# The first routing's operations two at a time in the second step beside attention A, its scatters one step earlier, and the second routing between the first expert tiles

## The reference

```
x = x + attn_a(layernorm(x))    # one head, rotary q and k, softmax, width 128
x = x + ffn(layernorm(x))       # 8 experts, each token goes to one of them
x = x + attn_b(layernorm(x))    # 16 heads of 64, causal
x = x + ffn(layernorm(x))       # the same experts again

def ffn(x):
    logits = x @ Wr + br
    idx = argmax(logits);  gates = softmax(logits)[idx]
    for ei in range(8):
        h = gelu(x @ W1[ei] + b1[ei]);  y = h @ W2[ei] + b2[ei]
        out += y * (gates where idx == ei)
```

## Time and profile before

| | |
|---|---|
| median of 3 runs | 865.49 us (863.0 to 867.37) |
| the profiled execution | 865.85 us, span from first to last instruction 863.5 us |
| busy: PE, DVE | 789.8 us (91%), 622.7 us (72%) |
| busy: ACT, POOL | 566.7 us (66%), 440.4 us (51%) |
| attention A with its loads | 0 to 122 us of the span |
| first experts | 123 to 226 us |
| attention B | 226 to 748 us |
| second experts | 748 us to the end |

### The profile page before, as it was taken

The page is one execution under the profiler, slowest core; times in us unless marked ns, Lnnn a source line. Parts: engine busy times, 40 slices in busy tenths (PEclk is TensorE's granted clock), DMA queues, the critical chain, the costliest instruction groups (busy, mean ns, idle before and its releaser), DMA issues.

```text
span 863.5 us, 24042 instructions
## 1 busy us (share of the span) xinstructions
PE 789.8 (91%) x6756; PEld 693.7 (80%) x6756; DVE 622.7 (72%) x2697; ACT 566.7 (66%) x2041; POOL 440.4 (51%) x771
## 2 busy tenths in 40 slices
PE   4999938999899999989999999999999999499992
PEld 3888827999778888878888888888778888399992
DVE  3889855666577777767777777887767776566664
ACT  1677645666577777767777777777767777266661
POOL 3334553677444454444544444544874544237772
PEclk9999957999999999999999999999999999889996
DMA  9920012313200000000000000000020000003135
GB/s 322 335 104 0 15 42 94 112 52 98 71 2 2 1 2 3 2 1 0 0 1 0 0 0 2 2 2 2 26 96 1 0 2 2 1 26 119 50 102 161
DMA packets 25928, 40.02 MB, mean 46 GB/s; under 512 B 4656, under 2 KB 17584, under 8 KB 24816
## 3 DMA queue, kind: packets, MB, share of 16 engines
q1 hardware_dynamic: 20848, 28.76, 10.4%
q0 software_dynamic: 4992, 10.27, 3.6%
HBM read 20.58 MB, written 18.43 MB: 45 GB/s over the span
## 4 chain that ended last, share of the span: by engine, by line
PE 75%; DVE 7%; POOL 7%; issue 6%; DMA 2%; ACT 1%; DVEq 0%; SPq 0%; POOLq 0%; ACTq 0%
PE PS L1151 11%; PE PS L1111 10%; PE PS L1163 10%; PE PS L1142 10%; PE PS L1120 9%; PE PS L1194 6%; PE PS L998 5%; PE PS L1000 5%; PE PS L999 5%; POOL xs_dram L323 2%; POOL w1b L356 1%; PE PS L1103 1%; PE PS L1048 1%; POOL pb L383 1%; POOL rstdA L318 1%
## 5 line engine op out<-in xcount | busy, mean ns | idle before, releaser
L381 POOL TENSOR_SCALAR pb<-pb,rib 128x128 f32<-128x128 f32 x256 | 96.1, 375 | 251.9 <-DVE rib L871 251.3
L862 DVE CUSTOM_DVE_ANT_0 PS<-PS,CST 128x128 f32<-128x128 f32 (+1 forms) x512 | 169.0, 381 | 65.3 <-PE PS L1163 62.0
L876 DVE COPY pT<-PS 128x384 f32<-128x384 f32 x256 | 139.7, 554 | 33.2 <-PE PS L1142 33.0
L522 ACT ACTIVATE pb<-PS,nbb 128x128 f32<-128x128 f32 x256 | 95.1, 371 | 102.4 <-DVE nbb L862 95.2
L496 ACT ACTIVATE yT<-PS,w1b 128x128 f32<-128x128 f32 x368 | 105.3, 369 | 64.8 <-PE PS L1111 64.8
L383 POOL TENSOR_SCALAR pb<-pb,rib 128x256 f32<-128x256 f32 x256 | 123.3, 482 | 0.0
L1142 PE MATMUL PS<-CST,pb 128*128 128x128 f32 x768 | 117.5, 279 | 4.4 <-POOL pb L383 3.6
L524 ACT ACTIVATE pb<-PS,nbb 128x256 f32<-128x256 f32 x256 | 121.4, 474 | 0.0
L339 POOL DMA_INDIRECT yt_dram<-XY x92 | 93.4, 1015 | 32.5 <-issue 19.7
L1142 PEld LDWEIGHTS PS<-CST,pb 128*128 128x128 f32 x768 | 85.8, 142 | 28.0 <-issue 15.3
L1151 PE MATMUL PS<-pT,vb 128*64 128x256 f32 (+1 forms) x1024 | 103.4, 339 | 1.9 <-DVE pT L876 1.6
(11 more groups left out here) (132 smaller groups left out, 1667.5 us busy)
## 6 DMA issues: line engine op xcount, KB each, us to landing
xs_dram<-XY SPq DMA_DIRECT2D x4, 1483.5 KB, 13.2
XY<-xs_dram SPq DMA_DIRECT2D x4, 1225.5 KB, 5.8
W1S<-in_W SPq DMA_DIRECT2D x1, 2048.0 KB, 21.3
W2S<-in_W SPq DMA_DIRECT2D x4, 512.0 KB, 8.3
out_dram<-X SPq DMA_DIRECT2D x8, 256.0 KB, 4.1
yt_dram<-XY POOLq DMA_INDIRECT x92, 2.4
XY<-xs_dram SPq DMA_DIRECT2D x4, 258.0 KB, 2.6
xs_dram<-TOK,POS POOLq DMA_INDIRECT x64, 2.4
```

The lines of the kernel that those rows point to most:

```text
L862: last = nc.vector.tensor_tensor_reduce(ps, ps, CST[:, m:m + c1 - c0], -SCALE_B, HIGHEST, ALU.add, ALU.min, nbb[:, hh % 4, c0 // P:c0 // P ...
L876: nc.vector.tensor_copy(pT[:, hh % 4, :], PS[:, bank, 0:3 * P]).then_inc(b_pT, 1)
```

## The change

The first routing's 28 operations are placed in two steps instead of three: 13 in step 13 (one at each of the first seven hooks, none at the eighth, two at each of the last three) and the other 15 in step 14, two at a time. POOL's wait for the routing moves from step 15 to step 14, and the scatters of group 0 are 2, 2, 3, 3, 3 and 3 in steps 14 to 19, with none in step 20. In the first expert layer the second routing gets the order that the second layer has: expert steps 0 to 6 behind every fourth operation; and the scatters of group 1 get the second layer's pace. The work itself is the same.

```diff
@@ gpsimd
             attn_a(ROUTE0_AT - 1, 0)
             for s in range(ROUTE0_AT, NB + 5):
                 attn_a(s, s % 2)
-                if s == ROUTE0_AT + 2:
+                if s == ROUTE0_AT + 1:
                     before_scatters(0)
@@ vector
-            def attn_a(s, u, parts=()):
+            def attn_a(s, u, parts=(), so_many=(0,) * HOOKS):
                 v = (u + 1) % 2
+                hook = iter(so_many)
 
                 def part():
-                    for _ in parts:
-                        return
+
+                    for _ in range(next(hook)):
+                        next(parts, None)
...
             parts = route(0)
-            for s in range(ROUTE0_AT - 1, NB + 5):
-                attn_a(s, s % 2, parts if s >= ROUTE0_AT else ())
-                if s == ROUTE0_AT + 2:
-                    for _ in parts:
-                        pass
+            attn_a(ROUTE0_AT - 1, 0)
+            attn_a(ROUTE0_AT, 1, parts, (1, 1, 1, 1, 1, 1, 1, 0, 2, 2, 2))
+            attn_a(ROUTE0_AT + 1, 0, parts, (2,) * HOOKS)
+            for _ in parts:
+                pass
+            for s in range(ROUTE0_AT + 2, NB + 5):
+                attn_a(s, s % 2)
                 if s >= NB + 1:
                     weight_parts(s - (NB + 1))
...
-SCATTERS_A = (0, 0, 2, 2, 3, 3, 3, 3)
+SCATTERS_A = (0, 2, 2, 3, 3, 3, 3, 0)
+
+HOOKS = 11
...
-STEP_BEHIND = ((22, 26, 28), (4, 8, 12, 16, 20, 24, 28))
-
-SCATTER_PACE = (tuple(2 + t for t in range(GT)), tuple(7 + 3 * t // 4 for t in range(GT)))
+STEP_BEHIND = ((4, 8, 12, 16, 20, 24, 28),) * 2
+
+SCATTER_PACE = (tuple(7 + 3 * t // 4 for t in range(GT)),) * 2
```

## The result

The changed kernel takes 868.19 us (866.06 to 871.03, 17 runs) and the kernel before 865.46 us (863.0 to 869.31, 17 runs, measured together): ratio 1.0034, 95% interval 1.0021 to 1.0047. By the ratio it is slower by 2.9 us (2.7 by the medians). The interval lies clear of no change, but the difference is smaller than the 0.5% that the prediction set as its border, so it counts as the same. The forecast was 869.7. The profiled execution has a span of 866.2 us for 863.5.

What follows compares the result with a forecast made beforehand. PE bounds the kernel nearly everywhere, DVE the routing steps of attention A; +5.4 to the second routing, -2.6 at the experts' start and +1.4 in the tiles make +4.2 us, 869.7 us on the median of 865.49, range 865.4 to 872.0.

Steps and rivals of the forecast that it cites:

- Step 13: Attention A's step 13 issues 13 routing operations for 11: +0.5 us (0.2 to 0.7).
- Step 14: Attention A's step 14 issues 15 routing operations for 11, ten ahead of the rotation: +2.2 us.
- The clock: PE's longer idle time in step 14 drops its clock to half, slowing step 15: +1.6 us.
- step 15's emptier hooks: Attention A's step 15 has six routing operations fewer, going from 5.8 to about 5.7 us: -0.1.
- the upper end: Clock stays low for the 5.2 us that the first experts need, costing 2.6 us instead of 1.6.
- The scatters: Step 16's third scatter delays POOL's power in step 17: +1.2 us (0.9 to 1.3).
- T: Start of the second routing, 123.04 us before the change, forecast to come 5.4 us later.
- The start of the experts: DVE waits 2.4 us for data; first expert matmul at T + 9.0 instead of T + 11.6: 2.6 us gained.
- The tiles: First expert tiles give back 1.1 us to routing operations between them and 0.3 us to close scatters.
- Sum: Whole kernel: +5.4 - 2.6 + 1.4 = +4.2 us.
- The two rivals that would have given less: Clock stays up in step 14: 868.1 us, chance 0.2; not slower, variance within 0.3 us: 865.5 us, chance 0.2.
- the first of them: Clock stays up in step 14 because PE's idle time stays short: +2.6, 868.1 us, chance 0.2.

Runs made afterwards that it cites:

- kernel with the pairs later: Changed kernel with step 14's last five routing operations moved from ahead of the row maximum to the hooks behind it; ratio 1.0030 to the kernel before.
- the filler: Changed kernel with 28 throwaway identity transposes on PE in its idle time between its work of steps 14 and 15; ratio 1.0046 to the kernel before.
- the routing part alone: Changed kernel with only attention A's routing and scatter change, the experts' order and pace as in the kernel before; ratio 1.0052 to the kernel before.

## Why the prediction was right

- **Step 13** (+0.5): 8.60 for 7.97, +0.6. Counted from X, the layer norm comes 0.2 us later, behind the operation that moved behind `nba`; the rotation's sum 0.5 later, behind the next hook's pair; the last hook's pair adds 0.1.
- **Step 14** (+2.2): +2.1. The variance came 0.9 us later for 1.1, and so did POOL's multiply counted from X (4.43 us for 3.57), and the small operation behind the rotation was held to its end. The kernel with the pairs later shows that the total is right and one reason in it is not: I put 0.7 us on the row maximum's lost cover and took the operations between the rotation and the row maximum as its cause. With these moved away the cover is lost all the same and the step is as long. That the ten ahead of the rotation are the cause is my reading of the rows. The Trainium skill, SBUF — State Buffer, section Who interferes with whom, has the rule for the hold (one of the two fully blocks, whichever comes second). The 1.03 us of L781 for its 0.17, and the 1.02 and 1.05 of `nbF` for 0.15, agree with it.
- **The clock** (+1.6, and -0.1 for step 15's emptier hooks): +0.8 together. It fell as forecast; the term was mis-sized. I took half of 3.2 us as lost in full; PE still idled in the first 0.5 of it, and against the filler step 15 lost 0.9. The other 2.9 us at half speed are 1.45 us of work by the same estimate; why only 0.9 of it shows, no run says. The execution of the routing part alone comes near the size that I had as the upper end (2.6): 8.0 us, +2.3 against the filler's 5.7.
- **The scatters** (+1.2): +1.24, step 17 from 6.52 to 7.76. Step 18 kept its length, 5.27 for 5.28, and so did the stretch from step 19's X to T, 6.84 for 6.83.
- **T** (+5.4): +4.9.
- **The start of the experts**: data 3.57 us behind T for 3.67, wait 2.32 for 2.4, first matmul T + 9.01 for T + 9.0. Gain 2.6, as said. Here the second layer was a faithful model of the first.
- **The tiles** (-1.1 and -0.3): four tiles on 9.88 us for 10.05, so -0.9; at attention B's first power -0.9 in all. The close scatters cost nothing more, and POOL caught up ahead of attention B (0.74 us idle at 224.73). The 0.5 that I had too much stands there.
- **Sum**: 4.9 - 2.6 + 0.9 = 3.2 us at attention B, for a forecast of 4.2 and a measured 2.9 over 17 runs. The two terms that were too large are the clock (0.7) and the tiles (0.5); the misses of steps 13 and 14 cancel.

The two rivals that would have given less fell at their own marks: the clock did fall, and the variance of step 14 came 0.9 us later, not within 0.3. The time alone couldn't have decided it: 868.19 us is what the first of them forecast (868.1), and only the clock rows and the filler's trace rule it out.

## What to carry to other kernels

Gaps of another stage take only so much work. Spread over three steps the 28 operations cost DVE's steps 20.2 us in all; in two steps and one without, the same three steps took 22.9 even with the clock kept up by the filler. Moving five of them to other gaps of step 14 changed its length by 0.05 us: how many there are decided, not where they stood. Before an indirect DMA is issued earlier, look at the issuing engine's idle time in front of its next critical instruction: here one more scatter cost 1.2 us in step 16, whose next power had no slack, and nothing in step 17, where POOL had 1.7 us of it. And a consumer moved ahead of its data only moves the wait; place it by the arrival that the trace shows.

## What the runs showed of the hardware

The same idle time of 3.9 us was followed by 3.4 us of half clock in one execution and by 6.8 us in another, so the cost of a fall, 0.9 and 2.3 us here, can't be read from one profile. With 2.85 us idle, in the kernel with the pairs later, the clock was low for 3.4 us too, and fell only some 0.9 us after PE had begun again (PE's row at 95.78; the window 96 to 97 shows 0.85, 97 to 100 show 0.50, 100 to 101 shows 0.94). Transposes of 3.2 us in all, whose results are thrown away, kept it up.
